# Plain attention of a ViT block on Trainium2: two semaphores of six counts for the query scores, and four fewer waits on TensorE

## The reference, cut to what matters

```
x  = layernorm(tokens) ; q, k, v = per-head projections   # 197 tokens, 12 heads of 16
att = softmax(q k^T / sqrt(16))                           # over all 197 keys
h   = tokens + att v
```

## The kernel before, in words

| loop | first instruction | instructions in the body |
|---|---|---|
| embed | 240 | 472 |
| plain attention | 1763 | 1786 (1596 loads and matmuls, 124 ALU_OP, 32 FUSED_REGOPS, 33 EVENT_SEMAPHORE, 1 branch) |
| causal attention | 5840 | 1747 |
| whole stream | | 11351 |

## Time and profile before

### The profile page before, as it was taken

The page is one execution under the profiler, slowest core; times in us unless marked ns, Lnnn a source line. Parts: engine busy times, 40 slices in busy tenths (PEclk is TensorE's granted clock), DMA queues, the critical chain, the costliest instruction groups (busy, mean ns, idle before and its releaser), DMA issues. The chain is left out here.

```text
span 4705.1 us, 159457 instructions
## 1 busy us (share of the span) xinstructions
PE 4417.1 (94%) x47156; PEld 3827.4 (81%) x47156; DVE 3407.1 (72%) x10266; ACT 2723.7 (58%) x7054; POOL 2053.1 (44%) x3346
## 2 busy tenths in 40 slices
PE   8999999889999999999997999999999799989978
PEld 7999999867787777787776888888888576679965
DVE  5666666678787788887775888888887688830067
ACT  3444444356666666666664555555555699954445
POOL 2232232333333333443344666666666466631145
PEclk9999999979999999999997999999999799999955
DMA  5667776677777777776656777777774233369977
GB/s 171 191 194 192 193 194 191 177 161 172 168 171 169 170 170 168 180 173 165 164 137 147 159 159 159 161 158 160 158 160 110 69 96 95 96 184 276 271 212 230
DMA packets 459820, 791.78 MB, mean 168 GB/s; under 512 B 80443, under 2 KB 330748, under 8 KB 459644
## 3 DMA queue, kind: packets, MB, share of 16 engines
q1 hardware_dynamic: 459644, 789.24, 67.5%
HBM read 519.59 MB, written 265.72 MB: 167 GB/s over the span
## 5 line engine op out<-in xcount | busy, mean ns | idle before, releaser
L693 DVE TENSOR_REDUCE a_mx<-a_sq 99x2 f32<-99x394 f32 x1536 | 831.7, 563 | 244.9 <-PE a_sq L762 218.6
L642 ACT ACTIVATE a_ex<-a_sk 99x792 f32<-99x792 f32 (+1 forms) x768 | 639.7, 833 | 212.1 <-PE a_sk L776 196.8
L1174 DVE TENSOR_REDUCE c_mx<-c_sq 99x2 f32<-99x198 f32 (+1 forms) x1536 | 660.2, 457 | 28.1 <-PE c_sq L1243 16.0
L1133 ACT ACTIVATE c_ex<-c_sk 99x792 f32<-99x792 f32 (+1 forms) x768 | 512.1, 667 | 288.6 <-PE c_sk L1261 262.1
L1081 POOL TENSOR_SCALAR_AFFINE_SELECT c_ex<-c_ex 99x396 f32<-99x396 f32 (+1 forms) x768 | 422.2, 550 | 405.9 <-ACT c_ex L1133 401.2
L762 PE MATMUL a_sq<-a_ks,a_qs 96*99 96x198 bf16 x3072 | 545.7, 260 | 22.2 <-DMA a_ks<-scr_qk 17.7
L393 PE MATMUL e_tokp<-e_wmap,e_xin 128*99 128x192 f32 x3072 | 551.6, 330 | 14.0 <-DVE e_junk L341 14.0
L393 PEld LDWEIGHTS e_tokp<-e_wmap,e_xin 128*99 128x99 f32 x3072 | 483.4, 167 | 14.5 <-issue 14.0
L776 PE MATMUL a_sk<-a_qs,a_ks 99*99 99x198 bf16 (+1 forms) x3072 | 406.2, 255 | 44.5 <-issue 44.5
L1243 PE MATMUL c_sq<-c_ks,c_qs 96*99 96x99 bf16 (+1 forms) x3072 | 441.5, 231 | 0.0
L762 PEld LDWEIGHTS a_sq<-a_ks,a_qs 96*99 96x99 bf16 x3072 | 331.1, 130 | 112.8 <-DVE a_mx L693 51.5
(11 more groups left out here) (207 smaller groups left out, 10842.6 us busy)
## 6 DMA issues: line engine op xcount, KB each, us to landing
e_xin<-in_x SPq DMA_DIRECT2D x128, 594.0 KB
x_w<-in_fc SPq DMA_DIRECT2D x128, 576.0 KB, 5.6
scr_tv<-e_tv SPq DMA_DIRECT2D x128, 297.0 KB
a_tv<-scr_tv SPq DMA_DIRECT2D x128, 297.0 KB
scr_tv<-a_res SPq DMA_DIRECT2D x128, 297.0 KB
c_tv<-scr_tv SPq DMA_DIRECT2D x128, 297.0 KB
scr_qk<-e_parts SPq DMA_DIRECT2D x128, 222.8 KB
scr_qk<-e_parts SPq DMA_DIRECT2D x384, 74.2 KB
```

What stands on the lines that cost most here:

```text
L642: nc.scalar.activation(ex[0:rows, g, kt].rearrange("p (a s) -> p a s", a=2), sk[k % 2][0:rows, :, 0:2 * SP], ACT.Exp).then_inc(exped.sem, 1)
L693: nc.vector.reduce_max(mx[:, b.parity, qt, h:h + 2], sq[f % 2][:, :, 0:SEQ], AX.X).then_inc(maxed.sem, 1)
L1133: nc.scalar.activation(to, of, ACT.Exp).then_inc(exped.sem, 1)
L1174: nc.vector.reduce_max(mx[:, b.parity, qt, h:h + 2], sq[f % 3][:, :, 0:SP if qt else TT], AX.X).then_inc(maxed.sem, 1)
```

## The change

Two semaphores of six counts, one for each PSUM bank, take the place of one of twelve, on PE and on DVE. PE's wait for the second key tile's exponential moves ahead of the whole value product, and the wait for the first goes. `key_scores` no longer waits for odd k. The wait for `o_copied` before `value_products(b5, 0)` goes. Nothing else is changed, and no operation on data is added, taken away or moved.

```diff
-        scored_q = m.event("a_scored_q", 12)
-        maxed = m.event("a_maxed", 12)
+        scored_q = [m.event(f"a_scored_q{i}", 6) for i in range(2)]
+        maxed = [m.event(f"a_maxed{i}", 6) for i in range(2)]
...
             def reduce(b, f):
                 qt, h = f // 6, 2 * (f % 6)
-                dve.wait_ge(scored_q.sem, scored_q.at(b, f + 1))
-                nc.vector.reduce_max(mx[:, b.parity, qt, h:h + 2], sq[f % 2][:, :, 0:SEQ], AX.X).then_inc(maxed.sem, 1)
+                dve.wait_ge(scored_q[f % 2].sem, scored_q[f % 2].at(b, f // 2 + 1))
+                nc.vector.reduce_max(mx[:, b.parity, qt, h:h + 2], sq[f % 2][:, :, 0:SEQ], AX.X).then_inc(maxed[f % 2].sem, 1)
...
             def query_scores(b, f):
 
                 qt, h = f // 6, 2 * (f % 6)
-                if f < 2:
-                    pe.wait_ge(maxed.sem, maxed.at(b - 1, 11 + f))
-                else:
-                    pe.wait_ge(maxed.sem, maxed.at(b, f - 1))
+                pe.wait_ge(maxed[f % 2].sem, maxed[f % 2].at(b, f // 2))
...
-                mm.then_inc(scored_q.sem, 1)
+                mm.then_inc(scored_q[f % 2].sem, 1)
...
-                if k < 2:
-                    pe.wait_ge(exped.sem, exped.at(b - 1, 5 + k))
-                else:
+                if k == 0:
+                    pe.wait_ge(exped.sem, exped.at(b - 1, 5))
+                elif not kt:
                     pe.wait_ge(exped.sem, exped.at(b, k - 1))
...
             def value_products(b, g):
 
+                pe.wait_ge(exped.sem, exped.at(b, 2 * g + 2))
                 for kt in range(2):
-                    pe.wait_ge(exped.sem, exped.at(b, 2 * g + kt + 1))
...
                 if b3.inside(n):
-                    pe.wait_ge(maxed.sem, maxed.at(b3))
+                    pe.wait_ge(maxed[1].sem, maxed[1].at(b3))
...
                 if b5.inside(n):
-                    if b6.inside(n):
-                        pe.wait_ge(o_copied.sem, o_copied.at(b6))
                     value_products(b5, 0)
```

More of the change, by code:

```diff
@@ L685, in _ @@
         def _(dve):
-            for e in (maxed, max_high, max_rest, recip, o_normed, left, h_rest):
+            for e in (*maxed, max_high, max_rest, recip, o_normed, left, h_rest):
                 e.seed(dve)
@@ L750, in _ @@
         def _(pe):
-            for e in (scored_q, max_turned, scored_k, summed, o_turned, h_turned, done):
+            for e in (*scored_q, max_turned, scored_k, summed, o_turned, h_turned, done):
                 e.seed(pe)
```

## The result

The changed kernel takes 4807.83 us (median of 4 runs, 4806.13 to 4808.54) against 4715.28 for the kernel before on the same chip: 1.0206 of it, 95% interval 1.0187 to 1.0224. It is 2% slower. Its profiled execution took 4806.13 us, 99.3 more than that of before.

What follows compares the result with a forecast made beforehand. PE, busy 94% of the span, was taken to set the pace, with instruction reloads at loop returns. 4706.9 - 74 (plain) + 137 (causal) = 4770 us profiled; with 11.5 for the median, 4781 us, range 4703 to 4832.

Steps and rivals of the forecast that it cites:

- The count: PE's stream: plain body 1786 to 1727 instructions, causal head to 5775, ALU_OP 124 to 81, EVENT_SEMAPHORE 33 to 21.
- The borders: Where PE's 256-instruction blocks begin: at 256k + p, with p put at 163 to 199.
- seven blocks against eight: PE's loop returns: a loop over seven blocks has room for the one fetched ahead; one over eight must reload.
- The plain loop: Plain attention loop: shortened body covers seven blocks instead of eight, so the reloads go, -74 us.
- Instructions and waits at 0: Both loops: the removed instructions, cut waits and later value-product wait taken as covered, 0 us, with up to 8 to be had.
- The causal loop: Causal attention loop: moved head makes it cover eight blocks; 19 late returns at 7.2 us, +137 us, bounds 127 to 181.
- Causal stays clean: Rival, causal loop: body length alone decides, so its returns stay near 208 ns; 4644 to 4636 us, 17%.
- Every other return: Rival, causal loop: ten stalls at 7.2 us, +72, with -74 from the plain loop; 4717 us, 14%.
- Nothing happens: Rival, both loops: plain keeps its reloads and causal stays clean; 4718 us within some 8, 7%.
- The two-page rule: Rival, both loops: only two pages are held, so every long return stalls and the time stays; 1% of the 7%.

Runs made afterwards that it cites:

- the placed kernels: Kernel before with 224 increments ahead of the plain loop and 24 more ahead of the causal: 4659.63 us; changed kernel with 56 ahead of the causal: 4638.72 us.
- the run with 120 ahead: Kernel before with 120 one-instruction semaphore increments on PE ahead of the causal loop: 4848.41 us, 1.0300 of before.
- with 20 ahead: Kernel before with 20 one-instruction semaphore increments on PE ahead of the plain loop: 4704.65 us, 0.9979 of before.

## Why the prediction was right

**The count.** The body of 1727 instructions, the plain head 1 earlier, the causal head at 5775: the compiled stream has all three, and between two plain branches the trace has 1727 instructions of PE, 81 ALU_OP, 28 FUSED_REGOPS and 21 EVENT_SEMAPHORE among them. The borders, which I had from two rows, were at 194, inside my 163 to 199. The step that everything hung on, seven blocks against eight, was right for both loops, and the runs with padding show it by moving the loops alone. The packets came to 215; I had said 216.

**The plain loop** gave 76.0 us, I had 74. The 2 come from the clean turn, 66.6 against 66.7 and 66.8. With the old body at a good place the turns are 66.6 as well (1265.6 / 19), so the 0.1 to 0.2 us by which clean turns were longer in the kernel before do not come from the 59 instructions or the waits; the clean turns there stood between late ones.

**Instructions and waits at 0.** Right: the placed kernels differ by 0.2 us in 2257.

**The causal loop: this term was mis-sized.** All 19 returns late, as I expected; but I put 7.2 us on each from the plain loop's turns, 137 in all, and they cost 8.9, 169.2 in all, inside the 127 to 181 that I gave as bounds. (I wrote that nine of the ten slow plain branches are followed by a turn in the stretch; all ten are. Their turns average 74.05 us against 66.77 for the nine clean ones, 7.3 more, so the 7.2 was right for the plain loop.) The step that failed is the carrying over of a price: a head 33 into its block has 223 instructions to run before it needs the next block, a head 205 in has 51. Both the table and the order of time show what that does: with 122 left (the run with 120 ahead) there is one gap and 7.4 us, with 51 left there are two and 8.9, with 2 left they meet in one wait of up to 10.3 us and cost 10.8. That the second gap is the wait for the block behind the head's is read from this series and from the packet that ends 1.3 to 1.9 us ahead of its end; a packet's row does not say which instructions it carries.

That my bounds held is in part luck. The upper one, 9.5, came from a plain turn with one gap of 4.55 us and a clock of 0.91, not from a second gap, and with the head 2 to 32 instructions ahead of a border instead of 51 the loop loses 202 to 206 us, outside them.

**The rest of the kernel** came 6.1 us later, for which I had no term. The profiled executions of two kernels that differ by four padding instructions lie 11 us apart (4637 and 4648), so I make nothing of it.

**The sum.** 4706.9 - 76.0 + 169.2 + 6.1 = 4806.1, where I had 4770 for this execution: 32 us too little in the causal price, 6 in the rest, 2 too much in the plain loop. The forecast for the median, 4781, is 27 short and not 36, since I had added 11.5 for how the median of before stood to its profiled execution, and here that is 1.7. Those 10 us are luck too.

**The rivals.** *Causal stays clean* needed the length alone to decide; the changed loop has the same 1747 instructions and went from 0 to 19 late. *Every other return* was not what it did, but the reason that I gave against it, the longer tail, is only part: with the branch 46 instructions behind the border returns still alternate, with 88 they don't. *Nothing happens* fell with the counts. The two-page rule of the Trainium skill ("Runtime: NRT & Kernel Launch", Instruction fetch mechanics) fell by more than one loop: bodies of 1786, 1747 and 1727 instructions all return in 0.2 us when they fit into seven blocks. What the same section says of such a branch, that its target has to be fetched before execution goes on, agrees: late branches take 3.5 to 6.6 us each.

**What stays open** is what decides between some late returns and all of them. A tail of 6 gives none or one, one of 88 and more gives all; between them the same tail of 26 to 28 gives 10, 15 or 19 as the head moves from 33 through 74 to 92 into its block, and 46 with the head at 53 gives every other one. In the kernel before, the first packet of a late turn starts 0.4 to 1.1 us after its branch, in the changed one with 60 ahead of the plain loop 0.2 to 0.9 us before every branch. That does not decide it either: with 20 ahead it starts 0.2 to 0.9 us before the late branches and every other return is clean, and with 120 ahead of the causal loop 0 to 1.4 us after, and all are late. Nor is it settled why the late branches of the changed kernel's causal loop come by fours: four of 4.9 to 5.5 us, four of 3.9 to 4.1, four of 5.1 to 5.6, four of 3.8 to 4.0, and so on, a cycle of eight returns. Nine packets a turn in a store of eight blocks would move the head's place by one each turn and give such a cycle, but no run tests that.

## What to carry to other kernels

Where a hardware loop's body is near a whole number of blocks, count the instructions ahead of it as well as in it: seven blocks or eight was worth 76 us in one loop and 169 in the other, and the edit itself nothing. The sign to look for is an engine that waits for "issue" just behind its loop branch, with branches of microseconds and packets on the queue of instructions in a turn that should need none. Eight blocks are not lost for certain: with the last border 6 instructions ahead of the branch none or one of 19 returns was late. Before a small edit is judged by its time, give the kernel back its old place with padding; and a kernel that is too long by a few instructions can be moved instead of shortened, as 56 to 60 increments made the changed kernel 1.5% faster than the kernel before.

## What the runs showed of the hardware

- PE's instructions come in blocks of 256 with borders at 256k + 194 (193 to 195) of this program's stream, labels not counted. The plain and the causal loop, wherever they covered seven blocks (bodies of 1727 to 1786 instructions), return in 207 to 231 ns, and after their first turn no packet comes in them.
- Cutting instructions out of a loop can slow down another loop behind it that is not touched, by 17%.
- A late return costs PE twice: a gap, and a lower granted clock behind it. In the changed kernel's causal loop the first gap is 3.3 to 5.2 us, and the mean clock of a turn 0.89 to 0.97, where it is 1.00 in clean ones. Each gap of over 0.3 us there ends 1.3 to 2.0 us behind the end of a packet of the instruction queue. Over the whole loop that was 96 us of idle time and 73 us of slower matmuls.
- Padding of 60 increments cost next to nothing where PE waits for its first data anyway: it moved the first branch of the kernel before's causal loop by 0.9 us ((2604.0 - 2415.5) - (2606.0 - 2418.4)), with 18.5 us of waits for a DMA ahead of it, and the changed kernel's plain one by 0.5 (1077.7 against 1077.2). In the changed kernel the same sixty moved the causal one by 11, with a clock that stayed at 0.50 for longer. 224 ahead of the plain loop outlast that wait: PE then stands 43.5 us for "issue" where it stood 17.7 for a DMA, and the first branch comes 25 to 26 us later.
